# Second attention: a shared piece for both heads' last 64 keys, and a two-part output product in groups of two turns

## The reference

```python
q = einsum('blh,ph->blp', hidden, Wq).reshape(B, L, 32, 64).transpose(0, 2, 1, 3)   # k, v alike
q, k = apply_rope(q, k, pos, pos)
for start in range(0, L, 128):                       # heads 0..29
    ks, ke = max(0, start - 64), start + 128
    s = einsum('bhqd,bhkd->bhqk', q[:, :, start:ke], k[:, :, ks:ke]) / 8
    s = where(qi >= ki, s, -inf)
    out_local.append(einsum('bhqk,bhkd->bhqd', softmax(s), v[:, :, ks:ke]))
# heads 30, 31: the same over all keys, causal
s = einsum('blp,hp->blh', concatenate([out_local, out_global]), Wo) + bo
x = x + s * silu(ffn(xn))
```

## Time and profile before

| | |
|---|---|
| timed runs, median of 3 | 3144.66 us (3143.03 to 3146.24) |
| profiled execution, span | 3149.4 us (no time besides the span is given for it) |
| TensorE busy | 3012.4 us, 96% |
| vector engine, ScalarE, GpSimd busy | 67%, 59%, 32% |
| granted TensorE clock, mean | 0.987 of full |
| 1800 to 1900 us: TensorE, vector engine, ScalarE, GpSimd | 100.00, 58.85, 57.43, 64.27 us of 100 |
| same, DMA share | 0.41 |

### The profile page before, as it was taken

One profiled execution on the slowest core, in us unless ns is written; L12 is line 12 of the kernel. 1 busy time (PEld: TensorE's weight loads), 2 busy tenths in 40 slices (PEclk: granted clock), 3 DMA queues, 4 the chain that ended last, 5 costly groups with the idle time before them and its releaser, 6 DMA issues. The chain is left out here.

```text
span 3149.4 us, 66407 instructions
## 1 busy us (share of the span) xinstructions
PE 3012.4 (96%) x23638; PEld 2264.0 (72%) x23638; DVE 2118.6 (67%) x5888; ACT 1863.2 (59%) x4638; POOL 1017.1 (32%) x1627
## 2 busy tenths in 40 slices
PE   7999999999999999997988999999999999999998
PEld 5888888853444444434877888788887888788886
DVE  5666666678989989975655555655556555555556
ACT  4666666647877778773445555455554555455553
POOL 0000000001100000001016666576656666566663
PEclk9999999989999999998999999999999999999999
DMA  4111111232333232103224444344443444244432
GB/s 150 50 48 48 48 48 41 60 68 44 69 50 64 35 75 45 30 9 116 83 69 110 99 101 94 103 122 101 94 107 93 114 103 95 67 114 105 102 87 68
DMA packets 296707, 246.35 MB, mean 78 GB/s; under 512 B 149180, under 2 KB 231740, under 8 KB 296252
## 3 DMA queue, kind: packets, MB, share of 16 engines
q1 hardware_dynamic: 296380, 242.11, 31.7%
HBM read 100.71 MB, written 44.04 MB: 46 GB/s over the span
## 5 line engine op out<-in xcount | busy, mean ns | idle before, releaser
L1838 ACT ACTIVATE b_pp<-b_pp,b_nm 128x192 f32<-128x192 f32 (+2 forms) x1024 | 472.8, 463 | 447.6 <-DVE b_nm L2005 366.1
L1007 ACT ACTIVATE a_pt<-ps 128x512 f32<-128x512 f32 x1024 | 556.1, 595 | 178.9 <-PE ps L1043 177.9
L176 DVE TENSOR_REDUCE mx<-ps 128x2 f32<-128x1024 f32 x512 | 622.3, 1224 | 58.6 <-PE ps L167 44.0
L1808 POOL TENSOR_SCALAR b_pp<-b_pp,b_rc 128x192 f32<-128x192 f32 x960 | 389.2, 428 | 383.9 <-DVE b_rc L2014 383.9
L2026 DVE COPY b_pt<-ps 128x384 f32<-128x384 f32 (+2 forms) x336 | 182.1, 556 | 316.7 <-PE ps L1927 301.4
L2005 DVE CUSTOM_DVE_ANT_0 b_pp<-ps,b_mk 128x192 f32<-128x192 f32 x960 | 276.3, 354 | 136.8 <-PE ps L1906 136.8
L797 DVE SCALAR_TENSOR_TENSOR f_yac<-ps,f_cw,f_yac 128x128 f32<-128x128 f32 x992 | 278.1, 344 | 125.3 <-PE ps L596 123.0
L596 PEld LDWEIGHTS ps<-w,f_sq 128*128 128x128 f32 x2048 | 265.2, 191 | 26.5 <-issue 6.0
L596 PE MATMUL ps<-w,f_sq 128*128 128x128 f32 x2048 | 270.2, 275 | 0.3
L1961 PE MATMUL ps<-b_wo,b_oT 128*128 128x256 f32 x1024 | 241.6, 380 | 3.7 <-ACT b_vv L1831 3.7
L1056 PE MATMUL ps<-a_pt,a_v 128*32 128x256 f32 x3072 | 242.0, 395 | 0.0
(11 more groups left out here) (282 smaller groups left out, 7332.8 us busy)
## 6 DMA issues: line engine op xcount, KB each, us to landing
b_rt<-b_qf SPq DMA_DIRECT2D x1024, 64.0 KB, 2.0
qk_parts<-f_aa SPq DMA_DIRECT2D x32, 512.0 KB, 2.7
v_rows<-f_va_ SPq DMA_DIRECT2D x16, 512.0 KB, 2.8
rl<-in_W1qT SPq DMA_DIRECT2D x64, 128.0 KB, 2.6
rl<-in_W1kT SPq DMA_DIRECT2D x64, 128.0 KB, 2.7
rl<-in_W1vT SPq DMA_DIRECT2D x32, 256.0 KB, 3.2
b_wo<-in_W1oT SPq DMA_DIRECT2D x16, 512.0 KB, 4.2
b_vs<-b_vv SPq DMA_DIRECT2D x60, 128.0 KB, 2.9
```

Source lines behind the costliest of these rows:

```text
L176: e.tensor_reduce(M["mx"][kh % 3][:, :, jt, h], P.pair(s), AX.X, ALU.max, negate=True).then_inc(P.free_sem(s), 1)
L1007: e.activation(pt[(4 * i + 2 * j + a) % 12][:, :], P.ap((*s, a)), ACT.Exp).then_inc(P.free_sem((*s, a)), 1)
L1808: m = e.tensor_scalar(x, x, r[:, 2 * u + h:2 * u + h + 1], 1.0, ALU.mult, ALU.mult)
L1838: e.activation(x, x, ACT.Exp, bias=nm[n % 4][:, c:c + 1], scale=-1.0, accum_out=sm[n % 4][:, c:c + 1]).then_inc(exp_done, 1)
```

## The change

- Head 1's keys are read in reversed order of 64-key chunks, so the middle transposed piece holds the last 64 keys of both heads. Only the later 64 queries of a block can see these, so its two products have 64 columns (`l0`, `l1`). The three transposes are placed so that the middle one's first 64 columns are overwritten, and the copy takes 320 columns instead of 384. Head 1 gets a mask of its own, `turned`.
- `vs` now has both heads' shifted values; `earlier` has six DMAs instead of four.
- The output product is made by `mm3` (6 matmuls of type FR a tile for two turns) in groups of two turns. `evac` writes a high part `oh`, and a new step `evac_low` on the vector engine writes the low part `ol` and releases bank 7. It stands behind the third `third`. The weights `wo` are loaded for two turns (in the middle of odd turns) and split by `wo_split` on ScalarE and GpSimd at their end.
- `side` gives out two tiles a local stride; stores come two at a time.
- `dynamic_dma_scratch_size=1024` is set.

```diff
                 out += evacs
-                evacs = []
             if u < len(turned):
                 out.append(turned[u])
+            if evacs and (u == 2 or len(slots) < 3):
+                out += [("evac_low", f[1]) for f in evacs]
+                lowered.update(evacs)
+                evacs = []
         out += evacs
+        out += [("evac_low", f[1]) for f in out if f[0] == "evac" and f not in lowered]
+        lowered.update(f for f in out if f[0] == "evac")
...
-            if store:
-                p.append(store.pop())
-            if side and (not last or j % 2):
+            p += store
+            store = []
+            for _ in range(min(len(side), j % 2 if last else 2)):
                 p.append(side.pop(0))
-                if p[-1][1] % 4 == 3:
+                if p[-1][1] % PB == PB - 1:
                     store.append(("store", *p[-1][1:]))
-        if at % 4 == 3:
-            p.append(("wo", n // 4))
-            side += [("out", n // 4, t) for t in range(NQ)]
+            if at % 2 and j == 0:
+                p.append(("wo", n // 2))
+        if at % 2:
+            p.append(("wo_split", n // 2))
+            side += [("out", n // 2, t) for t in range(NQ)]
...
-        oT = sb("oT", [128, NP // 2, L])
-        wo = [sb(f"wo{i}", [128, 4, 256]) for i in range(2)]
+        oh, ol = (sb(f"o{x}", [128, 4, L], FR) for x in "hl")
+        wr = sb("wr", [128, 2, 256])
+        woh, wol = ([sb(f"wo{x}{i}", [128, 2, 256], FR) for i in range(2)] for x in "hl")
...
                         w.wait_ge(pv_done, pt_end[vb_before(n)])
                     x, at = vb_of(n) % 2, n % 2 * 128
-                    e.dma_start(vs[x][0:64, 1:NQ, :], v[64:128, 0:NQ - 1, at:at + 64]).then_inc(vb_in[x], 16)
-                    e.dma_start(vs[x][64:128, :, :], v[0:64, :, at:at + 64]).then_inc(vb_in[x], 16)
+                    e.dma_start(vs[x][0:64, 1:NQ, 0:64], v[64:128, 0:NQ - 1, at:at + 64]).then_inc(vb_in[x], 16)
+                    e.dma_start(vs[x][64:128, :, 0:64], v[0:64, :, at:at + 64]).then_inc(vb_in[x], 16)
+                    e.dma_start(vs[x][0:64, :, 64:128], v[0:64, :, at + 64:at + 128]).then_inc(vb_in[x], 16)
+                    e.dma_start(vs[x][64:128, 1:NQ, 64:128], v[64:128, 0:NQ - 1, at + 64:at + 128]).then_inc(vb_in[x], 16)
                     e.dma_start(vb[x][0:64, :, 0:64], v[64:128, :, at:at + 64]).then_inc(vb_in[x], 16)
-                    e.dma_start(vb[x][64:128, 1:NQ, 64:128], v[64:128, 0:NQ - 1, at + 64:at + 128]).then_inc(vb_in[x], 16)
+                    e.dma_start(vb[x][64:128, :, 64:128], v[64:128, :, at + 64:at + 128]).then_inc(vb_in[x], 16)
...
-                    if n >= 2:
-                        w.wait_ge(*P.filled(("out", n - 2, NQ - 1)))
-                    e.dma_start(wo[n % 2][:, :, :], wo_t[:, n % 4 * 4:n % 4 * 4 + 4, :]).then_inc(wo_in[n % 2], 16)
-                    if n % 4 == 3:
+                    w.wait_ge(wo_low, n)
+                    e.dma_start(wr[:, :, :], wo_t[:, n % PB * 2:n % PB * 2 + 2, :]).then_inc(wo_in, 16)
...
+                elif k == "wo_split":
+                    w.wait_ge(wo_high, n + 1)
+                    if n >= 2:
+                        w.wait_ge(*P.filled(("out", n - 2, NQ - 1)))
+                    e.tensor_tensor(wol[n % 2][:, :, :], wr[:, :, :], woh[n % 2][:, :, :].bitcast(F32),
+                                    ALU.subtract).then_inc(wo_low, 1)
...
+                elif k == "wo_split":
+                    w.wait_ge(wo_in, 16 * (n + 1))
+                    if n >= 2:
+                        w.wait_ge(*P.filled(("out", n - 2, NQ - 1)))
+                    e.activation(woh[n % 2][:, :, :], wr[:, :, :], ACT.Copy).then_inc(wo_high, 1)
...
-                        if t >= 8:
-                            w.wait_ge(*P.filled(("out", t // 4 - 2, 4 * half + 3)))
-                        e.activation(oT[:, t % 8, half * CH:(half + 1) * CH], P.ap(o),
-                                     ACT.Copy).then_inc(P.free_sem(o), 1)
+                        if t >= 4:
+                            w.wait_ge(*P.filled(("out", t // 2 - 2, 4 * half + 3)))
+                        e.activation(oh[:, t % 4, half * CH:(half + 1) * CH], P.ap(o),
+                                     ACT.Copy).then_inc(oh_ready, 1)
...
-                                m = e.matmul(scores(u, h), q[r, d:d + 128], kk[r, d:d + 192], start=True, stop=True)
+                                keys = kk[r, d:d + 192]
+                                if h:
+
+                                    keys = keys.rearrange("p (c k) -> p c k", c=3)[:, ::-1, :]
+                                m = e.matmul(scores(u, h), q[r, d:d + 128], keys, start=True, stop=True)
...
-                        for c in range(3):
-                            at = 384 * s[2] + 128 * c
-                            m = e.transpose(P.ap(f)[:, c * 128:(c + 1) * 128], pp[n % 3][:, at:at + 128], ident[:, :])
-                        m.then_inc(P.full_sem(f), 1)
+                        y, at = P.ap(f), 384 * s[2]
+                        e.transpose(y[:, 192:320], pp[n % 3][:, at + 128:at + 256], ident[:, :])
+                        e.transpose(y[:, 0:128], pp[n % 3][:, at:at + 128], ident[:, :])
+                        e.transpose(y[:, 128:256], pp[n % 3][:, at + 256:at + 384],
+                                    ident[:, :]).then_inc(P.full_sem(f), 1)
...
-                            e.matmul(o0, vs[x][:, i + u, :], y[:, 0, :], start=u == 0, stop=False)
-                            e.matmul(o1, v[:, i + u, right + 64:right + 128], y[:, 2, :], start=u == 0, stop=False)
-                            e.matmul(o0, vb[x][:, i + u, 0:64], y[:, 1, :], start=False, stop=u == 3)
-                            e.matmul(o1, vb[x][:, i + u, 64:128], y[:, 1, :], start=False, stop=u == 3).then_inc(pv_done, 1)
+                            l0, l1 = o0[:, 64:128], o1[:, 64:128]
+                            e.matmul(o0, vs[x][:, i + u, 0:64], y[:, 0, :], start=u == 0, stop=False)
+                            e.matmul(o1, vs[x][:, i + u, 64:128], y[:, 1, :], start=u == 0, stop=False)
+                            e.matmul(l0, vb[x][:, i + u, 0:64], y[:, 2, 0:64], start=False, stop=u == 3)
+                            e.matmul(l1, vb[x][:, i + u, 64:128], y[:, 2, 0:64], start=False, stop=u == 3).then_inc(pv_done, 1)
...
-                    w.wait_ge(wo_in[n % 2], 16 * (n // 2 + 1))
-                    w.wait_ge(*P.emptied(("o", 4 * n + 3, t // 4)))
-                    for c in range(4):
-                        m = e.matmul(P.ap(s)[:, 0:256], oT[:, n % 2 * 4 + c, t * 128:(t + 1) * 128], wo[n % 2][:, c, :],
-                                     start=c == 0, stop=c == 3)
+                    w.wait_ge(wo_low, n + 1)
+                    w.wait_ge(*P.emptied(("o", 2 * n + 1, t // 4)))
+                    for c in range(2):
+                        x = (slice(None), n % 2 * 2 + c, slice(t * 128, (t + 1) * 128))
+                        m = mm3(e, P.ap(s)[:, 0:256], oh[x], ol[x], woh[n % 2][:, c, :], wol[n % 2][:, c, :],
+                                c == 0, c == 1)
...
-                                mask = mk[:, L - 192:L] if i + u else mk0[:, :]
+                                if h:
+                                    mask = turned[:, 0 if i + u else 1, :]
+                                else:
+                                    mask = mk[:, L - 192:L] if i + u else mk0[:, :]
...
-                            lo, hi = 0, 384
+                            lo, hi = 0, 320
...
+                elif k == "evac_low":
+                    t, i = strides[n]
+                    if not whole(t) or i % 4 == 3:
+                        o, half = ("o", t, i // 4), i // 4
+                        at = (slice(None), t % 4, slice(half * CH, (half + 1) * CH))
+                        w.wait_ge(oh_ready, 2 * t + half + 1)
+                        e.tensor_tensor(ol[at], P.ap(o), oh[at].bitcast(F32), ALU.subtract).then_inc(P.free_sem(o), 1)
```

More of the change, by code:

```diff
@@ L26 @@
 ACT_TURNS = (0, 1, 2, 3)
+PB = NP // 2
 class Waits:
@@ L1540, in second_attention_plan @@
         for f in fourths(at):
-            p += [f, ("evac", f[1])]
+            p += [f, ("evac", f[1]), ("evac_low", f[1])]
         if at < s:
@@ L1630, in second_attention @@
         vb = [sb(f"vb{i}", [128, NQ, 128]) for i in range(2)]
-        vs = [sb(f"vs{i}", [128, NQ, 64]) for i in range(2)]
+        vs = [sb(f"vs{i}", [128, NQ, 128]) for i in range(2)]
         pp = [sb(f"pp{i}", [128, 2 * L]) for i in range(3)]
         pt = [sb(f"pt{i}", [128, 4, 128]) for i in range(5)]
-        oT = sb("oT", [128, NP // 2, L])
-        wo = [sb(f"wo{i}", [128, 4, 256]) for i in range(2)]
+        oh, ol = (sb(f"o{x}", [128, 4, L], FR) for x in "hl")
+        wr = sb("wr", [128, 2, 256])
+        woh, wol = ([sb(f"wo{x}{i}", [128, 2, 256], FR) for i in range(2)] for x in "hl")
         acc = sb("acc", [128, NQ, 256])
@@ L1646, in second_attention @@
```

(8 more changed lines are left out.)

26 lines of the change are left out of this document (15 added, 11 removed).

## The result

| | before | after |
|---|---|---|
| median of the timed runs | 3144.48 us (3143.03 to 3146.24, 4 runs) | 3217.84 us (3213.30 to 3226.47, 4 runs) |
| span of the profiled execution | 3149.4 us | 3212.5 us |
| granted TensorE clock, mean | 0.987 | 0.976 |

The ratio is 1.0241, interval 1.0228 to 1.0255: 73 us slower, where +38 was forecast (3183 us). The time lies above the range.

What follows compares the result with a forecast made beforehand. TensorE's queue was taken as the bound, with vector-engine and SyncE chains close behind. Terms -18 + 5 + 53 - 2 = +38 us on the 3149.4 span gave 3187, less 4.7 from span to median: 3183 us, range 3132 to 3215.

Steps and rivals of the forecast that it cites:

- the boundaries' term: Strides after the three batch boundaries: late gates and a late store cost 17.8 us each, +53 us, bounds 25 and 62.
- TensorE waits 5.7 us, in three strides: After each batch boundary, transposes wait for normalizations behind GpSimd's gates on late-fetched rows: +15.1 us a boundary.
- 3.4 us of TensorE: Next batch's group 0: first tile waits for tile 6's store, the vector engine holds the reductions; stride +2.7 us.
- The order of the chain: At boundaries: ropes issued, store, fetch, landing, gates, two normalizations; transposes may start at 10.2 us, due at 4.5.
- Steady turns: Local turns: first stride 11.1 us, second 10.19; 21.29 against 21.69, -0.40 a turn, -18 us over about 45.
- x: Gain a stride from the shared piece's products streaming 64 instead of 128 columns: 0.37 us, kept between 0 and 0.42.
- rival C: Short matmuls save nothing, x = 0: 60 second strides lose 0.37 each, +22 us, 3205 us; chance 0.11.
- rival E: Three-record output product costs as much a record as the old one, 0.23 us: 3253 us; chance 0.02.
- the second chain: Vector engine's transpose copy, sin multiply, cos multiply, next `first`: grows from 10.03 to 10.19 us, floor of local strides.
- The start: Turns 0 to 3, without output product, go from 2 x 10.03 = 20.06 us a turn to 21.29: +5 us.
- Rival A: Fetched rows arrive in time after boundaries, leaving only the wait for tile 6's store: 3139 us; chance 0.10.
- B: Weights land in time, both strides of a turn run at 10.19 us: 3142 us; chance 0.09.

Runs made afterwards that it cites:

- Run 6: Changed kernel plus six unread 512-column matmuls ahead of TensorE's wait for GpSimd in nine boundary strides: 3209.97 us, ratio 1.0198.
- Run 1: Changed kernel with SyncE's stores and their fetches put ahead of a stride's steps instead of behind them: 3152.73 us, ratio 1.0017.
- run 2: Changed kernel with the weight loads put ahead of the six copies of values at a turn's start: 3167.33 us, ratio 1.0069.
- run 5: The change's shared piece alone, with the output product and order of the kernel before: 3145.05 us, ratio 1.0005.
- Run 9: The shared piece alone with the old product, plus weight loads ahead of the six copies: 3088.83 us, ratio 0.983.
- run 7: Changed kernel with the shared piece's two products streaming 128 columns instead of 64: 3241.67 us, ratio 1.0309.
- run 10: Changed kernel with stores and weight loads first, plus evac_low ahead of the third transpose's copy: 3082.42 us, ratio 0.9816.

## Why the prediction was wrong

The direction, the places and the chain of waits were as forecast; one mechanism, the clock, was left out, and so the boundaries' term was mis-sized. That is the miss: +53 predicted, 26.1 + 25.8 + 26.6 = +78.5 measured. By its own steps, for one boundary (measured at the first, against undisturbed strides):

| | predicted | measured |
|---|---|---|
| transposes late in three strides | 3 x 5.7 = 17.1 | 5.3 + 5.8 + 7.0 = 18.1 |
| store wait in the fourth | 3.4 | 2.6 |
| first tile of the group waits for its low part | 0 ("the next wait covers it") | 0.5 |
| TensorE at 1.2 GHz after each of the four waits | not considered | 6.9 + 1.5 = 8.4 |
| four shorter strides | -2.6 | -2.8 |
| sum | 17.9 | 26.8 (26.1 against before's own four, of which the first took 11.63) |

- The failed step is "TensorE waits 5.7 us, in three strides" (and "3.4 us of TensorE" in the fourth): each wait was priced at its length. In the 5.3 us behind it TensorE ran at 0.50 to 0.66 of its clock, which cost 1.6 to 2.7 us apiece, 20 us for nine waits, and 4 us in the fourth strides. Run 6 shows it: with the idle time filled the clock stays at 1.00 and 20.0 us go.
- The order of the chain (ropes, store, fetch, landing, gate, normalizations) came out nearly to the number: transposes expected at 10.2, seen at 9.7, 10.3 and 11.5. Run 1 shows that this chain is the cause.
- Steady turns: -0.40 expected, -0.37 measured against the mean before (-0.29 against an undisturbed turn), -17 us in 46 turns for -18. Second strides 10.19 expected, 10.16 seen; first strides 11.1, seen 11.25. The sources were right: six copies ahead of the weights (runs 2, 5, 9).
- x was 0.37, measured 0.41 (run 7): rival C, no saving from short products, is excluded. The projections' record spacing carried over to the output product, which excludes rival E too.
- The floor of 10.19, "the second chain", was 10.16. Without it TensorE alone takes 10.13, not 10.07 (run 10), so the vector engine's low part cost 0.03 us a stride, not 0.12. Moving it paid through the first tile's 0.46 us.
- The start cost +10, not +5: turns 0 to 3 took 85.8 us before and 95.8 after. The 20.06 us a turn hold for turns 2 and 3 alone. Turns 0 and 1 took 17.9 and 27.8 before, 22.6 and 30.9 after, and run 2 takes 83.2 for the four, so this is the late weight load as well. In the span it does not show, because the second attention happened to begin at 1635.8 instead of 1642.6; over all profiled kernels this start scatters from 1635.4 to 1644.1.
- The carry from span to median: before, the profiled execution lay 4.9 above its median, after, 5.3 below. I carried -4.7 over; that is 10 us of the miss of 35. The span's 25 are the boundaries; the start's 5 more and the earlier beginning nearly cancel.
- Rival A (rows in time) and B (weights in time) failed in the changed kernel, but runs 1 and 2 are these two, made by hand: 3152.7 and 3167.3 against my 3139 and 3142, both together 3092.6 against 3098.
- `dynamic_dma_scratch_size=1024` was never run by itself. Run 9 has it, and its local strides are all 10.42 or 10.43, so it is not what lengthens strides.

## What to carry to other kernels

When a change raises the rate at which a stage makes its results, look at the transfers that feed and empty it: their place in the issuing queue was right for the old rate, and here one list entry's position was worth 65 us and another's 51. Price a TensorE wait of some 5 us at a third to a half more than its length, because it works at 1.2 GHz afterwards; waits of 2 to 2.5 us cost 1.5 us more in some places and nothing in others. A copy that is "only a DMA" takes its issue time from whatever stands behind it in the same queue: two of them cost as much here as the halved products saved.

## What the runs showed of the hardware

- After TensorE waits of 5.1 to 6.8 us the granted clock of the next 5.3 us was 0.50, 0.62 and 0.50 in one boundary's three strides, and 512-column records came every 0.43 us instead of 0.23. Matmuls without use in the gap kept it at 1.00.
- Shorter waits did it too, but not always: behind 2.47 us (change) it was 0.53 for 2 us, behind 1.83 and 2.10 us (run 6) 0.86 and 0.85 over the next stride, behind 1.89 us (change) and 2.19 us (run 5) it was 1.00.
- Pairs of products side by side in the array's column halves repeat after 0.06 us with 64 moving columns and after 0.11 with 128: no floor was met down to 64.
